# Self-attention: a head's two tiles of probabilities added on GpSimd and VectorE ahead of the matrix of ones, with shifted work in cross-attention and the FFN

## The reference

```python
x = _layernorm(x + _L0_attn_ref(x, ...))              # x: (16, 256, 512)
x = _layernorm(x + _L0_xattn_ref(x, ctx_2048, ...))
x = _layernorm(x + _L0_ffn_ref(x, L0_ffn_w_gating, L0_ffn_w_linear))

def _L0_attn_ref(x, ...):                             # 16 heads of 32
    q, k, v = (_split(lora_linear(x, W, b, Bm, Am)) for ...)
    scores = jnp.einsum('bhqd,bhkd->bhqk', q, k) * SCALE
    attn = jax.nn.softmax(scores, axis=-1)
    out = jnp.einsum('bhqk,bhkd->bhqd', attn, v)
    return lora_linear(out.transpose(0, 2, 1, 3).reshape(B, L, H * hd), Wo, bo, Bo, Ao)

def _L0_xattn_ref(x, c, ...):                         # channels 256, 512 positions, 16 heads of 16
    q = jnp.einsum('oc,bct->bot', Wq, x) + bq[None, :, None]   # k and v likewise from c
    p = jax.nn.softmax(jnp.einsum('bhkt,bhks->bhts', q, k) * SCALE, axis=-1)
    out = jnp.einsum('bhts,bhks->bhkt', p, v).reshape(B, H * K, T)
    return jnp.einsum('oc,bct->bot', Wo, out) + bo[None, :, None]
```

## Time and profile before

| | |
|---|---|
| median of 3 runs | 1977.44 us (1976.67 to 1979.93) |
| the profiled execution | 1983.12 us, its span 1981.2 us |
| granted TensorE clock, mean | 0.972 |
| busy: PE, DVE, ACT, POOL | 1900.6, 1495.3, 1124.2, 981.4 us |
| self-attention | up to about 740 us in the span |
| cross-attention | about 740 to 1615 us |
| FFN | from about 1615 us |

### The profile page before, as it was taken

The page is one execution under the profiler, slowest core; times in us unless marked ns, Lnnn a source line. Parts: engine busy times, 40 slices in busy tenths (PEclk is TensorE's granted clock), DMA queues, the critical chain, the costliest instruction groups (busy, mean ns, idle before and its releaser), DMA issues.

```text
span 1981.2 us, 31819 instructions
## 1 busy us (share of the span) xinstructions
PE 1900.6 (96%) x11460; PEld 1056.7 (53%) x11460; DVE 1495.3 (75%) x2632; ACT 1124.2 (57%) x2117; POOL 981.4 (50%) x968
## 2 busy tenths in 40 slices
PE   7999999999999898999999999999999899999997
PEld 4677777777777544444444444444444334444443
DVE  3566666666675667788888888888888439999997
ACT  3345444444444526888888888888887653333330
POOL 3455546555465423444444445445443237666664
PEclk9999999999999869999999999999999879999999
DMA  5665565655646521334443333334343300111111
GB/s 169 173 165 142 145 166 134 158 140 141 171 117 165 141 78 40 120 111 125 138 141 112 106 108 107 111 104 119 119 120 118 131 28 12 44 43 43 65 43 43
DMA packets 149899, 220.56 MB, mean 111 GB/s; under 512 B 41847, under 2 KB 50551, under 8 KB 148999
## 3 DMA queue, kind: packets, MB, share of 16 engines
q1 hardware_dynamic: 140078, 216.96, 38.0%
q10 hardware_dynamic: 9664, 1.58, 0.5%
HBM read 83.95 MB, written 32.02 MB: 59 GB/s over the span
## 4 chain that ended last, share of the span: by engine, by line
PE 65%; DVE 14%; DMA 7%; POOL 6%; issue 3%; SPq 2%; ACT 2%; ACTq 0%; DVEq 0%; POOLq 0%
PE bank L1287 9%; PE bank L1322 9%; PE bank L1616 8%; PE bank L85 7%; PE bank L86 6%; PE bank L87 6%; PE bank L1330 5%; PE bank L1592 5%; PE bank L577 4%; DMA xa_den<-inv 3%; PE bank L631 2%; DVE sa_mneg L703 2%; PE bank L644 2%; DVE sa_xnat L717 2%; DVE xa_mneg L1365 2%
## 5 line engine op out<-in xcount | busy, mean ns | idle before, releaser
L1365 DVE TENSOR_REDUCE xa_mneg<-bank 128x1 f32<-128x512 f32 x1024 | 643.7, 683 | 134.3 <-PE bank L1330 132.5
L1186 ACT ACTIVATE xa_prob<-bank 128x512 f32<-128x512 f32 x1024 | 549.0, 605 | 88.0 <-PE bank L1322 84.8
L1330 PE MATMUL bank<-xa_kst,xa_qst 48*128 48x512 f32 x1024 | 386.0, 462 | 14.5 <-DMA xa_kst<-xa_part_k 8.9
L1322 PE MATMUL bank<-xa_qst,xa_kst 49*128 49x512 f32 x1024 | 367.4, 447 | 15.5 <-ACT xa_prob L1186 15.2
L468 ACT ACTIVATE sa_prob<-bank 128x512 f32<-128x512 f32 x256 | 152.2, 598 | 333.7 <-PE bank L631 332.9
L1322 PEld LDWEIGHTS bank<-xa_qst,xa_kst 49*128 49x128 f32 x1024 | 167.5, 188 | 305.1 <-ACT xa_prob L1186 248.1
L1287 PE MATMUL bank<-xa_prob,xa_v 128*32 128x512 f32 x2048 | 280.0, 619 | 0.0
L1524 POOL TENSOR_TENSOR ff_total<-ff_prod,ff_mag 128x512 f32<-128x512 bf16 x128 | 194.3, 1518 | 96.7 <-DVE ff_mag L1640 96.7
L1330 PEld LDWEIGHTS bank<-xa_kst,xa_qst 48*128 48x128 f32 x1024 | 165.4, 188 | 55.5 <-DVE xa_mneg L1365 37.4
L703 DVE TENSOR_REDUCE sa_mneg<-bank 128x2 f32<-128x512 f32 x256 | 164.1, 682 | 35.1 <-PE bank L644 34.9
L1568 ACT ACTIVATE ff_gelu<-bank 128x512 bf16<-128x512 f32 x128 | 75.7, 593 | 156.7 <-PE bank L1616 156.7
(11 more groups left out here) (191 smaller groups left out, 3626.9 us busy)
## 6 DMA issues: line engine op xcount, KB each, us to landing
xa_qst<-xa_part_q SPq DMA_DIRECT2D x192, 128.0 KB, 3.5
xa_kst<-xa_part_k SPq DMA_DIRECT2D x192, 128.0 KB, 2.8
sa_qst<-sa_part_qh SPq DMA_DIRECT2D x64, 256.0 KB, 4.1
sa_kst<-sa_part_kh SPq DMA_DIRECT2D x64, 256.0 KB, 5.4
xa_den<-inv SPq DMA_DIRECT2D x64, 256.0 KB
sa_xraw<-xT SPq DMA_DIRECT2D x32, 256.0 KB, 4.3
sa_qst<-sa_part_ql SPq DMA_DIRECT2D x32, 256.0 KB, 4.0
sa_kst<-sa_part_kl SPq DMA_DIRECT2D x32, 256.0 KB, 5.8
```

Source lines behind the costliest of these rows:

```text
L1186: act.activation(prob[place[e]][:, :], banks[eb[e]][:, :], ACT.Exp, scale=X_SCALE)\
L1322: pe.matmul(banks[eb[e]][:, :], kst[u % 3][rows_of, head // 2, t * P:(t + 1) * P], qst[u % 3][rows_of, head // 2, :], start=True, stop=Tru ...
L1330: pe.matmul(banks[mb[m]][:, :], qst[u % 3][rows_of, n // 8, t * P:(t + 1) * P], kst[u % 3][rows_of, n // 8, :], start=True, stop=True).the ...
L1365: dve.tensor_reduce(mneg[:, u % 2, column:column + 1], banks[mb[m]][:, :], AX.X, ALU.max, negate=True).then_inc(s_mfree, 1)
```

## The change

1. **Sums of probabilities.** In units 0 to 27 (`SUMMED = U - 4`) the two tiles of a head's probabilities are added before the matmul with ones: POOL adds those of the first three heads of a half-unit, DVE that of the fourth (`add_both`), each one step after the head's exponential. The matmul with ones then runs over the sum alone: four matmuls for a half-unit in place of eight, and it waits for POOL (`s_three`) and DVE (`s_fourth`). The sums lie in the memory of the cross-attention's weights, whose load now waits for unit 27 (`Left.weights`).
2. **Cross-attention.** The conversions of x and c are cut in two instructions, at slots -14 and -11 for x and 0 and 5 for c; POOL's follow one slot later. The statistics are taken three slots after the output tile's addition, and POOL's scale five slots after it.
3. **The FFN's first turn** comes behind slot 1032, not 1022; its loads of x2 (`load(1)`, `load(2)`) come with its fifth turn, not its second. `down` waits for each hidden tile by itself.

```diff
+    both = mem("weights").sb("sa_both", [P, 2, SG, L], F32)
...
+    SUMMED = U - 4
...
+    def add_both(engine, wait, u, n):
+        b, j, e = n // SG, n % SG, S * u + n
+        wait.wait_ge(s_merged, DC * len(MERGE))
+        wait.wait_ge(s_exp, e + 1)
+        wait.wait_ge(s_av, 2 * (u - 1) + b + 1)
+        return engine.tensor_tensor(both[:, b, j, :], prob[:, e % PROBS, 0, :], prob[:, e % PROBS, 1, :], ALU.add)
...
         for slot in SLOTS:
             yield
+            if (un := unit(slot, EXP_AT + 1)) and un[0] < SUMMED and un[1] % SG < 3:
+                add_both(pool, wait, *un).then_inc(s_three, 1)
...
-            for of_ones in (False, True):
+            for t in range(2):
+                for j in range(SG):
+                    h = (u % SG) * SG + j
+                    pe.matmul(od[32 * j:32 * j + 32, 0:L], v[(u // SG) % 2][:, 2 * b + t, h * SDH:(h + 1) * SDH],
+                              prob[:, (S * u + SG * b + j) % PROBS, t, :], start=(t == 0), stop=(t == 1))
+            if u < SUMMED:
+                wait.wait_ge(s_three, 3 * (2 * u + b + 1))
+                wait.wait_ge(s_fourth, 2 * u + b + 1)
+                for j in range(SG):
+                    last = pe.matmul(od[32 * j:32 * j + 32, L:2 * L], ones[:, :], both[:, b, j, :],
+                                     start=True, stop=True)
+            else:
                 for t in range(2):
                     for j in range(SG):
...
+            if (un := unit(slot, EXP_AT + 1)) and un[0] < SUMMED and un[1] % SG == 3:
+                add_both(dve, wait, *un).then_inc(s_fourth, 1)
...
         def weights(wait):
-            wait.wait_ge(s_merged, DC * len(MERGE))
+            wait.wait_ge(s_av, 2 * SUMMED)
...
+    HIGH_AT = {"x": (-14, -11), "c": (0, 5)}
...
-        act.activation(xh[:, :, :], x1[b % 4][:, :, :], ACT.Copy).then_inc(s_hi, 1)
...
+        act.activation(xh[:, i, :], x1[b % 4][:, i, :], ACT.Copy).then_inc(s_hi, 1)
...
-            for job in jobs_in.get(slot - 2, []):
+            for i in range(CC):
+                if (b := batch(slot, HIGH_AT["x"][i] + 1)):
+                    low_x(pool, wait, b, i)
+                if (b := batch(slot, HIGH_AT["c"][i] + 1)):
+                    low_c(pool, wait, b, i)
+            for job in jobs_in.get(slot - 5, []):
...
-                    wait.wait_ge(s_pjfree, n + 1)
-                    dve.bn_stats(stats[:, t, :], x[:, t, :]).then_inc(s_bn, 1)
+            for job in jobs_in.get(slot - 3, []):
+                if job[0] == "o":
+                    _, b, t = job
+                    wait.wait_ge(s_pjfree, at[job] + 1)
+                    dve.bn_stats(stats[:, t, :], x1[b % 4][:, t, :]).then_inc(s_bn, 1)
...
-        yield
+        for _ in range(4):
+            yield
         left.stacks(wait, 2)
         load(1)
         load(2)
...
-            wait.wait_ge(s_hq, HT * (p + 1))
...
             for h in range(HT):
+                wait.wait_ge(s_hq, HT * p + h + 1)
...
-FFN_AT = [1022, 1046, 1070, 1078, 1086, 1094, 1108]
+FFN_AT = [1032, 1046, 1070, 1078, 1086, 1094, 1108]
```

More of the change, by code:

```diff
@@ L205, in self_attention_phase @@
     s_e, s_exp, s_av, s_od = s.sem("e"), s.sem("exp"), s.sem("av"), s.sem("od")
+    s_three, s_fourth = s.sem("three"), s.sem("fourth")
     s_sums, s_inv, s_back, s_den = s.sem("sums"), s.sem("inv"), s.sem("back"), s.sem("den")
@@ L960, in load_c, with high_x @@
     def load_c(sp, wait, b):
[L961 to L962 removed]
+        wait.wait_ge(s_hi, 4 * b)
+        wait.wait_ge(s_low, 4 * b)
         sp.dma_start(craw[:, :, :], rows(a["c"], b)).then_inc(s_c, 16)
[L965 removed]
+    def high_x(act, wait, b, i):
         wait.wait_ge(s_x1[b % 4], 16 * (b // 4 + 1))
@@ L1089, in gpsimd @@
         yield
-        low_x(pool, wait, 0)
+        for i in range(CC):
+            low_x(pool, wait, 0, i)
         yield
-        low_c(pool, wait, 0)
+        for i in range(CC):
+            low_c(pool, wait, 0, i)
         yield
@@ L1125, in gpsimd @@
                     .then_inc(s_ol, 1)
-            if (b := batch(slot, -13)):
-                low_x(pool, wait, b)
-            if (b := batch(slot, 1)):
-                low_c(pool, wait, b)
-            for job in jobs_in.get(slot - 2, []):
+            for i in range(CC):
+                if (b := batch(slot, HIGH_AT["x"][i] + 1)):
[3 more added lines that the diff above has]
+            for job in jobs_in.get(slot - 5, []):
                 if job[0] == "o":
@@ L1157, in scalar @@
         yield
-        high_x(act, wait, 0)
+        for i in range(CC):
+            high_x(act, wait, 0, i)
         high_w("k")
         yield
-        high_c(act, wait, 0)
+        for i in range(CC):
+            high_c(act, wait, 0, i)
         high_w("v")
@@ L1232, in scalar @@
                        .then_inc(s_y, 1)
-            if (b := batch(slot, -14)):
-                high_x(act, wait, b)
-            if (b := batch(slot, 0)):
-                high_c(act, wait, b)
+            for i in range(CC):
+                if (b := batch(slot, HIGH_AT["x"][i])):
+                    high_x(act, wait, b, i)
+                if (b := batch(slot, HIGH_AT["c"][i])):
+                    high_c(act, wait, b, i)
     def tensor(pe):
@@ L1259, in project_part @@
             else:
-                wait.wait_ge(s_hi, 2 * b + (1 if name == "q" else 2))
-                wait.wait_ge(s_low, 2 * b + (1 if name == "q" else 2))
+                wait.wait_ge(s_hi, 4 * b + (2 if name == "q" else 4))
+                wait.wait_ge(s_low, 4 * b + (2 if name == "q" else 4))
             if i == 0:
@@ L1493, in sync @@
         load(2)
-        for _ in range(PRELUDE - 2 + 2 * HT):
+        for _ in range(PRELUDE - 5 + 2 * HT):
             yield
```

24 lines of the change are left out of this document (9 added, 15 removed).

## The result

The changed kernel took **1966.05 us** (median of 4 runs, 1965.65 to 1969.52), the kernel before 1978.68 on the same chip. The ratio is 0.9935, with an interval of 0.991 to 0.996: 12.9 us faster (8 to 18), a third of the 38.5 us that were forecast, and above the range. The profiled execution took 1966.28 us, its span is 1964.5.

A forecast was written before the change was run, and what follows sets the result against it. TensorE (PE), 96% busy, was taken to set the pace, so a microsecond off its queue is worth a microsecond. Terms -12 - 15 - 7 - 4.5 = -38.5 us off the 1977.44 median gave 1939 us, range 1918 to 1960.

The forecast's parts named there:

- the ones' 24.3 us: Self-attention, PE: half the matmuls with ones go, 0.43 us in each of 56 half-units, 24.3 us gained.
- The adds on DVE: Self-attention: two adds a unit, 0.38 us each, fit DVE's 5.3 us of idle; charged only where the PE's ones wait.
- POOL's adds: Self-attention: six adds a unit, 0.73 us each, put at nothing; 5 us lost if their cover is gone.
- The stall at the ones: Self-attention, second half-units: in 9 of 28 units the ones wait for DVE's late add, 9 x (1.0 + 0.38) = 12 us.
- Self-attention in sum: Whole self-attention phase: -24 + 12 = -12 us, bounds -24 (no stall) and +12.
- rival 1: Self-attention gives nothing: adds block on POOL or DVE more often, stalls of 24 to 36.5 us, 1950 to 1962; chance 0.17.
- Cross-attention: -15: Cross-attention, statistics moved: 0.5 us gained twice in each of 15 undisturbed batches, 15 us; bounds nothing and 33.
- The three-step place: Cross-attention, three PE steps at an output tile's addition: 3.16 us against 2.05 plain; 0.5 of the lost 1.1 regained.
- The conversions by tile: Cross-attention, conversions of x and c halved: cost a bit more in total, put at nothing.
- Rival 3: Everything hidden well: no self-attention stall, whole 1.1 us back in cross-attention, whole transfer stall gone; 1910 us, chance 0.07.
- The load: FFN weights' transfer moved from step 1022 to 1032: 13.4 - 6 = 7 us gained, with a new stall of about 4 us.
- The last down projection: End of the kernel: PE starts as hidden tiles come, not after all 16; 4.5 us gained, bounds 3.4 and 5.5.

## Why the prediction was wrong, step by step

- **The step that failed first: the ones' 24.3 us taken as time.** The size was right (eight records fewer in 56 half-units, 0.43 us each). But "Nothing else is removed from the PE" was read as "24 us are gained", by the first paragraph's "a microsecond taken out of it is worth a microsecond". Alone they are worth 7 (3 to 11). The PE's 96% busy share hid that in this stage it often waits for DVE's reduces by a hair; with less work in front of them it waits longer for them, 10.6 us for 6.1, and its clock falls more often. The rows were there: 29 PEld waits for the reduces.
- **The adds on DVE: charged only where the ones wait.** I set their cost to 9 x (1.0 + 0.38) us, because DVE idles 5.3 us in a unit. Alone and unread, the add costs 16 us (10 to 21): it stands ahead of reduces that the PE waits for, at the ones or not, and these waits grow from 6.1 to 10.7 us; the rest of the 16 isn't located. The 5.3 us that DVE idles in a unit are spent waiting for its inputs, and weren't room for the add.
- **POOL's adds: "I put them at nothing", 5 us if the cover is gone.** They cost 9 (6 to 13). POOL's queue was still under the PE's time, as said. The rows show DVE's operations from SBUF meeting POOL's more often, and a wait for fraw of 39.9 us for 35.0; that the whole cost runs through DVE is inferred.
- **The stall at the ones: 12 us in nine half-units.** Measured 19.8 in 15, the mechanism as read from the earlier trace rows.
- **Self-attention in sum:** -12 forecast, +11.5 measured. That is rival 1 at its upper bound, +12, but not by its mechanism: it needed 36.5 us of stalls at the tight adds, and there are 19.8. The unread adds show that they cost without any stall there. The parts don't add up (-7 and +29 against +11.5): the adds with the ones halved cost less than beside the full ones. Why is open.
- **Cross-attention: -15.** The statistics' move is worth 1.2 us a batch in the timeline (twice 0.60), 18 us in 15 batches, where I had 1.0. The three-step place regained 0.93, not 0.5; 0.33 came back as a cost behind bn_stats. The conversions by tile at nothing: right within 5 us. (Rival 3 takes cross-attention at 25 us, where "the whole 1.1 us back" is 33 by the term's own bound: its sum would be 1902, not 1910.)
- **What wasn't priced: the last two tiles beside the FFN**, 7 us. The text followed the moved scale on POOL in cross-attention, not among the FFN's turns, where three steps are several turns of other work.
- **The load: -7**, measured -7, with the named new stall (4 us forecast, 3.4 and 4.9 measured).
- **The last down projection: -4.5**, measured 4.9 in the trace; it wasn't run alone, but other pairs of traces, which differ in more than it, give 4.9 to 5.3.

By the parts run alone: +11.5 - 8 - 0.6 - 7 - 4.9 = -9, against -12.9 (8 to 18) measured. The error of the sum is 24 us in self-attention. The rest, -26.5 forecast and -25.5 measured in one kernel, is right in its parts but for two: that the unpriced 7 us of the tail and the better gain in cross-attention offset one another is luck.

## What to carry to other kernels

Before work is moved from a busy engine to two half-idle ones, ask whom the busy engine waits for: if it is one of the two, an operation put in that queue costs time even when nobody waits for its result (here 56 adds of 0.61 us, 34 us of DVE's time, cost 16 us), and much of the saved work can be returned as waiting. A quick way to learn what a saving is worth is to leave the work out and add nothing: here that ceiling was 7 us of 24, against 29 for the adds. A step moved by a fixed number of turns has to be followed where the turns of two phases interleave as well.

## What the runs showed of the hardware

The cross-attention code is the same in the kernel before and in the experiments on self-attention, and its stretch from first to last exponential still took between 863.5 us (DVE's unread add, 754.9 to 1618.4) and 873.8 (all unread adds, 774.0 to 1647.8). Most of the difference lies at its end. The kernel before and self-attention's part alone need 846.5 and 846.3 us to their 1001st exponential, and 873.6 and 867.0 to their last: the last 23 take 27.1 us in the one and 20.7 in the other. There the PE is over 90% busy by the records in either case, but the granted clocks differ. The kernel before, up to its last exponential at 1614.2:

```profile
1590.00:1614.00 24.00, 23.48 (x75) 8.13 (x75) 0.25 (x1) 14.50 (x27) 3.81 (x3) 0.50 0.11 35
```

Self-attention's part alone, with its last exponential at 1620.3:

```profile
1591.00:1615.00 24.00, 22.61 (x110) 8.34 (x113) 2.13 (x5) 21.72 (x43) 5.75 (x8) 0.97 0.11 35
```

0.50 is the 1.2 GHz level, 0.97 nearly all 2.4. Nothing in the code differs there; only what came ahead was shifted. In sum it makes up to 10 us: more than several of the effects studied here, and the reason why a single trace's end doesn't settle them. Self-attention scatters too: with its code unchanged, cross-attention's first exponential stands at 735.8 to 744.4 us in the seven traces. And inside self-attention the halved ones alone brought more stretches at 0.93, beside longer waits of the PE; that the waits bring them is inferred.
